# Per-tile weight copies of an expert layer: from VectorE into four buffers to the transfer engines into eight, issued by SyncE

## The reference, cut to what matters

```python
logits = xf @ Wr.T + br                       # xf: 8192 tokens of 128
expert_idx = jnp.argmax(logits, axis=-1)
h = jax.nn.relu(jnp.einsum('td,efd->etf', xf, W1) + b1[:, None, :])     # 128 -> 512
y = jnp.einsum('etf,edf->etd', h, W2) + b2[:, None, :]                  # 512 -> 128
out = y[expert_idx, jnp.arange(xf.shape[0])]
```

## Time and profile before

| | |
|---|---|
| median of 3 runs | 955.97 us (955.83 to 957.16) |
| the profiled execution's own time | 956.35 us |
| its span in the profile | 954.6 us |
| PE busy in the span | 906.6 us |
| DVE busy in the span | 745.8 us |
| mean granted PE clock | 0.998 |

### The profile page before, as it was taken

How to read it: one execution, slowest core, us unless ns; L and a number is a source line. 1 busy time by engine, 2 the same in 40 slices (tenths; PEclk the granted TensorE clock), 3 DMA queues, 4 the chain that set the end, 5 groups by cost and what they waited for, 6 DMA issues and landing times.

```text
span 954.6 us, 30726 instructions
## 1 busy us (share of the span) xinstructions
PE 906.6 (95%) x11238; PEld 788.0 (83%) x11238; DVE 745.8 (78%) x2524; ACT 693.6 (73%) x1671; POOL 459.0 (48%) x1094
## 2 busy tenths in 40 slices
PE   3899999999999999999999999999999999899997
PEld 2688888788878887888888888888888878898997
DVE  4666788888878888888888888888888978877553
ACT  2777777777777777777777777777777766676664
POOL 4333333354545444544445454545453544777554
PEclk9999999999999999999999999999999999999999
DMA  6742000000000000000000000000000012245310
GB/s 177 222 131 43 2 2 2 3 13 3 10 5 11 5 8 7 8 8 8 7 8 8 8 8 7 8 8 8 7 8 7 8 41 72 65 96 108 96 52 21
DMA packets 45193, 31.44 MB, mean 33 GB/s; under 512 B 11555, under 2 KB 40166, under 8 KB 45046
## 3 DMA queue, kind: packets, MB, share of 16 engines
q1 hardware_dynamic: 39446, 19.93, 8.8%
q0 software_dynamic: 4320, 8.50, 2.8%
q10 hardware_dynamic: 1280, 1.05, 0.3%
HBM read 17.75 MB, written 12.17 MB: 31 GB/s over the span
## 4 chain that ended last, share of the span: by engine, by line
PE 68%; DVE 15%; ACT 8%; POOL 4%; issue 4%; DMA 0%; DVEq 0%; POOLq 0%; SPq 0%; ACTq 0%
PE ps L1652 9%; PE ps L1605 9%; PE ps L1580 7%; PE ps L1698 6%; PE ps L1396 5%; PE ps L1567 5%; PE ps L1559 5%; PE ps L1398 5%; PE ps L1397 5%; DVE sumsq L1292 4%; PE ps L1657 3%; PE ps L1682 2%; ACT probs L593 2%; ACT qk_hat L606 2%; PE ps L1435 1%
## 5 line engine op out<-in xcount | busy, mean ns | idle before, releaser
L1324 DVE TENSOR_TENSOR qk_hat<-ps,rstd 128x512 f32<-128x512 f32 x168 | 106.4, 685 | 50.1 <-POOL rstd L835 50.1
L1292 DVE TENSOR_REDUCE sumsq<-qk_hat 128x8 f32<-128x512 f32 x168 | 107.8, 678 | 34.6 <-ACT qk_hat L606 33.5
L828 POOL TENSOR_TENSOR rs_t<-rs_y 128x32 f32<-128x32 f32 x73 | 17.5, 240 | 234.7 <-ACT rs_y L647 234.7
L1605 PE MATMUL ps<-v_x,prob 128*64 128x65 f32 x2048 | 127.9, 225 | 2.1 <-ACT w_all L617 0.4
L1605 PE MATMUL ps<-v_c,prob 128*64 128x65 f32 x2048 | 124.3, 222 | 0.0
L1396 PE MATMUL ps<-w_hi,xc_hi 128*128 128x512 f32 x272 | 121.6, 447 | 2.3 <-POOL xc_lo L802 2.3
L666 ACT ACTIVATE prob<-ps,neg_shift 128x512 f32<-128x512 f32 x128 | 88.4, 691 | 48.6 <-PE ps L1652 48.6
L606 ACT ACTIVATE qk_hat<-ps 128x512 f32<-128x512 f32 x168 | 98.7, 599 | 33.5 <-PE ps L1398 27.9
L1605 PEld LDWEIGHTS ps<-v_x,prob 128*64 128x64 f32 x2048 | 105.0, 137 | 20.9 <-issue 19.3
L1652 PE MATMUL ps<-qT_all,kT_all 64*128 64x128 f32 x1536 | 111.6, 285 | 2.9 <-ACT w_all L617 1.2
L1398 PE MATMUL ps<-w_hi,xc_lo 128*128 128x512 f32 x272 | 108.0, 397 | 0.0
(11 more groups left out here) (241 smaller groups left out, 2248.2 us busy)
## 6 DMA issues: line engine op xcount, KB each, us to landing
x_res<-sorted_rows SPq DMA_DIRECT2D x71, 65.5 KB
w_all<-in_L_ffn_W_dram SPq DMA_DIRECT2D x16, 256.0 KB, 5.0
sorted_rows<-fill SPq DMA_DIRECT2D x8, 327.5 KB, 7.4
out_dram<-prob,x_res POOLq DMA_INDIRECT x71, 2.3
sorted_rows<-stage,idx POOLq DMA_INDIRECT x64, 2.4
ctx_res<-in_ctx_dram SPq DMA_DIRECT2D x8, 115.5 KB
x_res<-in_x_dram SPq DMA_DIRECT2D x1, 768.0 KB
sorted_rows<-fill SPq DMA_DIRECT2D x1, 524.0 KB, 4.7
```

Source lines behind the costliest of these rows:

```text
L1292: nc.vector.reduce_sum(sumsq[:, n * H:(n + 1) * H], sq[:, n * INNER:(n + 1) * INNER].rearrange("p (h d) -> p h d", d=DH), AX).then_inc(ss_ ...
L1324: nc.vector.tensor_tensor(qk_hat[:, n * INNER:(n + 1) * INNER].rearrange("p (h d) -> p h d", d=DH), ps_qk[:, n, :].rearrange("p (h d) -> p ...
L1605: last = nc.tensor.matmul(dst[half:half + DH, :], prob[:, kt, col + half:col + half + DH], v, start=kt == 0, stop=kt == 1)
```

## The change

DVE's copy (L902) and its semaphore `w1_set` are taken out. SP now issues one transfer for each tile, from `w1_all` to `w1_now` inside the on-chip memory, in a new function `weights`, which reads the tile's expert from `texp_i` by a `value_load` of its own. There are eight buffers (`HELD`): the two of `w1_more` first, two in `qk_hat`, and four in `v_c`, which the attention rounds use until their end too. The transfer waits for the relu of tile k - 8. PE's first product waits for the transfer (`weights_in`) by the semaphores `ld_exp`. ACT's loop over the last tiles is written for eight tiles in a turn in place of four, since the buffer's number must be known.

In SP's list the copies stand so: 0 and 1 ahead of the first 41 loads, 2 to 25 behind them, then the wait for `PAD_R` and the eight fills, then 26 to 38, then the wait for `TABLE_R` and the scatters, then loads 41 to 43, and from there for each k from 39 on one load (k + 5, while there is one) and one copy (k).

```diff
+BEFORE_PADS, BEFORE_TABLE = 26, 39
...
-        w1_now = [qk_hat[:, 0:W1C], qk_hat[:, W1C:2 * W1C], w1_more[:, 0, :], w1_more[:, 1, :]]
+        w1_now = ([w1_more[:, 0, :], w1_more[:, 1, :], qk_hat[:, 0:W1C], qk_hat[:, W1C:2 * W1C]]
+                  + [v_c[:, n, :, :].rearrange("p h e -> p (h e)")[:, 0:W1C] for n in range(4)])
+        HELD = len(w1_now)
...
+        def weights_in(eng, k):
+            eng.wait_ge(ld_exp[k % HELD], 32 + 16 * (k // HELD + 1))
...
+            def weights(lo, hi):
+
+                for k in range(lo, hi):
+                    e = sp.value_load(texp_i[0:1, k:k + 1], min_val=0, max_val=E - 1)
+                    if k == 2:
+                        sp.wait_ge(sim_done, 4 * B)
+                    if k == 4:
+                        sp.wait_ge(pv_done, B)
+                    past(sp, "relu_done", k - HELD)
+                    sp.dma_start(w1_now[k % HELD], flat(w1_all[:, bass.ds(e, 1), :])).then_inc(ld_exp[k % HELD], 16)
+
             sp.wait_ge(s["routed"], FIRST_R)
+            weights(0, 2)
             for half in (0, 1):
                 sp.wait_ge(sent[half], 32 * EARLY)
             load_part(0, NA)
+            weights(2, BEFORE_PADS)
 
             sp.wait_ge(s["routed"], PAD_R)
             for e in range(E):
...
+            weights(BEFORE_PADS, BEFORE_TABLE)
             sp.wait_ge(s["routed"], TABLE_R)
             for half in (0, 1):
                 sp.wait_ge(sent[half], 8 * B)
-            load_part(NA, T)
+            load_part(NA, NA + 3)
+            for k in range(BEFORE_TABLE, T):
+                if k + NA + 3 - BEFORE_TABLE < T:
+                    load_part(k + NA + 3 - BEFORE_TABLE, k + NA + 4 - BEFORE_TABLE)
+                weights(k, k + 1)
...
@@ VectorE, prep @@
-                    past(dve, "relu_done", k - 2)
-                    nc.vector.tensor_copy(w1_now[n], flat(w1_all[:, bass.ds(e, 1), :])).then_inc(se["w1_set"], 1)
@@ TensorE, tile @@
-                    past(pe, "w1_set", k)
+                    weights_in(pe, k)
```

More of the change, by code:

```diff
@@ L297, in whole @@
         s = {n: sem("m_" + n) for n in names}
-        tile_names = ("w1_set", "t_set", "T_done", "t_copied", "h_done", "relu_done", "y_done", "xb_set", "fin")
+        tile_names = ("t_set", "T_done", "t_copied", "h_done", "relu_done", "y_done", "xb_set", "fin")
         se = {n: sem("e_" + n) for n in tile_names}
@@ L535, in _, with tile @@
                 act.dma_start(to, src).then_inc(ld_w, 16)
-            def tile(k, four=0, inside=False):
+            def tile(k, eight=0, inside=False):
                 if inside or has_tile(k + 1):
-                    past(act, "T_done", k + 4 * four + 1)
+                    past(act, "T_done", k + 8 * eight + 1)
                     if k == -1:
@@ L544, in tile @@
                 if inside or has_tile(k):
-                    past(act, "h_done", k + 4 * four)
+                    past(act, "h_done", k + 8 * eight)
                     for c in range(C):
                         last = nc.scalar.activation(h_t[k % 4][:, c, :], ps_h[k % 2][:, c * P:(c + 1) * P], ACT.Relu,
-                                                    bias=w1_now[k % 4][:, F + c:F + c + 1])
+                                                    bias=w1_now[k % HELD][:, F + c:F + c + 1])
                     last.then_inc(se["relu_done"], 1)
@@ L710, in _ @@
             rounds_written_out(run)
-            at, turns = NA, (T - 1 - NA) // 4
+            at, turns = NA, (T - 1 - NA) // 8
             for k in range(REST[0], at):
@@ L714, in _ @@
             with act.Fori(0, turns) as turn:
-                for n in range(4):
+                for n in range(8):
                     tile(at + n, turn, True)
-            for k in range(at + 4 * turns, T + 1):
+            for k in range(at + 8 * turns, T + 1):
                 tile(k)
@@ L1556, in tile @@
                     past(pe, "t_copied", k)
-                    past(pe, "w1_set", k)
+                    weights_in(pe, k)
                     for c in range(C):
-                        last = nc.tensor.matmul(ps_h[k % 2][:, c * P:(c + 1) * P], w1_now[k % 4][:, c * P:(c + 1) * P],
+                        last = nc.tensor.matmul(ps_h[k % 2][:, c * P:(c + 1) * P], w1_now[k % HELD][:, c * P:(c + 1) * P],
                                                 t_t[:, k % 4, :], start=True, stop=True)
```

## The result

The changed kernel takes 1017.6 us (median of 4, 1013.8 to 1019.1), the kernel before 955.9 beside it: a ratio of 1.0636, 95% interval 1.0624 to 1.0649. Forecast were 1015, with a range of 1002 to 1026. The profiled execution is the fastest of the four, 1013.8 us.

A forecast was written before the change was run, and what follows sets the result against it. PE bounds the kernel on average, but SP's issuing decides this change: 956.35 + 32.4 + 13.2 + 14.2 (three waits) + 2 (clock) - 2 (DVE) = 1016.2 us, 1015.8 against the median, stated as 1015, range 1002 to 1026.

The forecast's parts named there:

- DVE is not what ends a wait: Woven rounds and last stage: dropping 30 us of DVE copies gains 2 us, ends 0 and 5.
- A copy's price on SP: SP's list: each of 71 copies takes 1.2 us to issue, ends 1.16 and 1.45.
- Landing: From a copy's issue to its arrival within on-chip memory: 3.0 us, ends 2.3 and 5.0.
- First wait: Ahead of tile 2: copy 2 stands behind 41 loads, PE loses 32.4 us, ends 31 and 35.
- Second wait: Ahead of tile 26: copy 26 queues behind the fills, PE loses 13.2 us, ends 8.4 and 15.
- Third wait: Tiles 39 to 65: SP's load and copy take 2.37 us against PE's 1.90; loss 14.2 us, ends 12.2 and 20.7.
- The clock: After the long waits PE's first tiles run at 1.2 GHz: 2 us, ends 0 and 6.
- the copies are hidden: Rival, whole tile stage: PE gains some of 5.3 us of gaps, 954 us; 2% faster, 1% no change.
- only the order matters: Rival, tiles 39 to 65: a pair takes SP under 1.9 us, third wait gone, 1001 us; chance 8%.
- the fills do not hold copy 26 back: Rival, tile 26: second wait 8.4 us, later waits absorb part of earlier ones, 1004 us; chance 14%.
- copies are dearer than loads: Rival, SP's list: a copy takes 1.45 us, a pair 2.62, 1026 us; chance 13%.
- the first wait is not there: Rival, ahead of tile 2: PE's position was misread, so 32 us less, 983 us; chance 4%.

The follow-up runs named there:

- e4: Kernel before with no copies, PE and ACT reading a fixed expert's weights from `w1_all`, choice of expert left out: 974.23 us, ratio 0.9971 to the kernel before.
- e7: SP copies only tiles 0 to 29, by turns with its loads, and DVE copies 30 to 70: 956.54 us, ratio 1.0004 to the kernel before.
- interleaved kernels: Changed kernel with 11 loads ahead of copy 2, then loads and copies by turns, run twice: 1003.98 and 1002.08 us, ratios 1.0256 and 1.0238 to kernel before.
- e6: Changed kernel with copies 26 to 29 moved ahead of the eight fills: 1009.61 us, ratio 1.0552 to the kernel before.
- e10: Changed kernel with copies 39 to 70 taking a fixed expert, without the table read: 1021.22 us, ratio 1.0433 to the kernel before.
- e11: Changed kernel with copies 39 to 70 cut to 8 of 516 numbers per partition, table read kept: 1028.07 us, ratio 1.0504 to the kernel before.
- second profile: Profile of the changed kernel run again with no edit: 1019.33 us, ratio 1.0658 to the kernel before.
- e2: Changed kernel with copies 39 to 70 taking a fixed expert, without the table read, an earlier run: 1023.42 us, ratio 1.0475 to the kernel before.
- e3: Kernel before with eight buffers and ACT's loop of eight tiles, copies still on DVE: 976.35 us, ratio 0.9989 to the kernel before.

## Why the prediction was right, point by point

- **DVE is not what ends a wait.** Right: 26.6 us of its time went without a gain; some 3 us are to be had (e4, 0.9 to 4.7). The 2 us taken off did not show: tiles 2 to 25 take 60.2 us, as before, and there the start at the low clock works against them. In e7, without the waits, tile 39 starts 1.7 us early. That is one profile against one, and 0.7 of it is there at tile 2 already, so that it comes from DVE's relief is not shown. It was spent at once on later fills.
- **A copy's price on SP.** 1.2 us forecast; 1.19 from copy to copy (copies 2 and 3: 1.70 us from the start of one to the end of the other, less 0.51 for the issue itself). A load takes (45.43 - 0.35)/40 = 1.13.
- **Landing.** 3.0 us forecast, 2.3 measured in the quiet stretch. The 0.7 us between them is the term's error. The estimate from the Trainium skill (DMA: Bandwidth & Descriptors, Anatomy of one DMA), 2.6, was nearer; the trace has 2.29.
- **First wait.** 32.4 forecast, 29.7 and 30.6 measured. In the first profile 0.6 us of the difference are the shorter landing, 1.4 the faster loads, and 0.7 the earlier start of the first load, at 775.92. The interleaved kernels show its cause.
- **Second wait.** 13.2 forecast, 12.6 and 15.4 measured: 8.2 us from copy 26's issue to its product. The rule on order within one issuing engine's transfers (the Trainium skill, DMA: Bandwidth & Descriptors, Queues, rings and completion order) chose the right one of the two prices. The trace agrees, with 8.2 and in e6 9.0 us from issue to product behind the fills against 2.4. It does not tell the order in the queue from transfer engines that are simply full: their share is 1.20 from 890 to 898.
- **Third wait.** 14.2 forecast, 12.3 and 13.7 measured, at 2.36 and 2.375 us a pair against 2.37. Of the difference, 0.7 us is the landing and about 1.1 the wait of 1.17 us that PE already had ahead of tile 39, which the table counts in the stretch before.
- **The clock.** 2 us forecast. It fell to 0.50 in both long waits. After the second one tiles 26 to 30 take 10.5 us against 8.6; after the first, tiles 2 to 25 take 60.2 us against 60.1, and a loss there cannot be told from DVE's gain.

The sum was 59.8 us over the profiled execution of before; measured are 57.5 and 62.6. That the forecast of 1015 comes so near to 1017.6 is in part luck: the three waits differ from their prices by up to 2.7 us downwards and 2.2 upwards, and the +2 for the clock and the -2 for DVE cancel without either having been measured by itself. The mechanism does not hang on that, since each wait stands in the trace at its place and with its releaser. The rivals: "the copies are hidden" fell with the first row, "only the order matters" with the 2.36 us a pair, "the fills do not hold copy 26 back" with the 8.2 us and e6, "copies are dearer than loads" with 1.19 us a copy, and "the first wait is not there" with PE's idle 30.86 us.

## What to carry to other kernels

An engine that only issues transfers shows no busy time in this profile and can still be full: count its instructions, here 1.1 to 1.2 us for each transfer whose address comes from a table, and hold that against the pace of whoever consumes it. When work is added to an in-order list, look first at what stands ahead of it (here 41 loads, 46 us) and at what is then pushed behind it (here the fills), before asking what the freed engine is worth. And 30 us taken from an engine that ends no wait were worth some 3, at most 4.7 by the interval of e4.

## What the runs showed of the hardware that was not expected

**PE's table reads are slower at a certain distance behind a copy within the on-chip memory.** The read of PE's list, L1547 in the kernel before, L1570 in e10 and L1571 in e11, each over the stretch behind the table: minimum, median, maximum ns.

```profile
L1547 PEldq TENSOR_LOAD <-table_texp_i x32: 295/300/431, 879.8 to 938.2; - x32
```

```profile
L1570 PEldq TENSOR_LOAD <-table_texp_i x26: 297/502/608, 946.9 to 1000.2; - x26
```

```profile
L1571 PEldq TENSOR_LOAD <-table_texp_i x26: 297/300/433, 946.1 to 1004.6; - x26
```

The median is 300 ns without copies and with short ones, 502 with full copies at 1.9 us each. Full copies at 2.36 and 2.375 us, in the changed kernel, leave it at 310 and 302, with 574 and 640 as the longest. The slow ones go by when a read starts. Between 1.0 and 1.45 us after SP issued a copy, all take 452 to 640 ns: 8 of 26 in the changed kernel, 5 of 26 in its second profile, 12 in e10. Of the 54 other reads of these three stretches five take over 360. In e2 all reads in that span are slow too, 503 to 657 ns, and so are seven that start from 0.7 to 1.65 us after an issue. That the reads meet the copy's data there is the likely reason; it was not tried.

**Two of the experiments' three chips had a slower last sixth.** On the chips of 977 us, tiles 2 to 25 take 68.1 us and tiles 26 to 39 take 38.9 in e3, where the kernel before takes 60.1 and 28.6 in its profile, and until 770 us the profiles agree. In all profiles of those chips DVE and ACT have waits after 784 that the trace ends by nothing on the core; in the profiles of the chip of 956 us, and in those of the kernel before and the changed kernel that the result rests on, there is none. Two rows of e4's waits (total us, times, longest):

```profile
DVE prob L917 <- remote: 9.8, 4, 4.5
ACT kT_all L548 <- remote: 7.1, 2, 5.1
```

What they wait for was not tried and stays open.
